# Stores in the third convolution, row terms between the two Hilbert products, and both copies of the mixed planes on ScalarE

## What is computed

```python
x = x + _L0_conv_ref(_gn(x), w_real, w_imag, b_real, b_imag)  # rfft2, complex 3x3 conv over frequencies + bias, irfft2
x = x + _L1_conv_ref(_gn(x))     # u, v: 8 channels each; gates: u . sum of v over rows > 0, v . sum of u over rows > 0
x = x + _L2_conv_ref(_gn(x), W)  # 3x3 convolution, 16 to 16 channels
x = x + _L3_conv_ref(_gn(x), weight)  # 3x3 convolution, 16 to 16 channels
```

## Time and profile before

| | |
|---|---|
| profiled execution, whole | 4709.38 us |
| its span, first to last instruction | 4707.6 us |
| median of three runs | 4704.55 us |
| PE busy | 4279.1 us, 91% |
| DVE busy | 3334.5 us, 71% |
| ACT busy | 2540.4 us, 54% |
| mean granted TensorE clock | 0.971 |

### The profile page before, as it was taken

One profiled execution on the slowest core, in us unless ns is written; L12 is line 12 of the kernel. 1 busy time (PEld: TensorE's weight loads), 2 busy tenths in 40 slices (PEclk: granted clock), 3 DMA queues, 4 the chain that ended last, 5 costly groups with the idle time before them and its releaser, 6 DMA issues.

```text
span 4707.6 us, 229463 instructions
## 1 busy us (share of the span) xinstructions
PE 4279.1 (91%) x85024; PEld 2675.9 (57%) x85024; DVE 3334.5 (71%) x13348; ACT 2540.4 (54%) x8637; POOL 1.0 (0%) x6
## 2 busy tenths in 40 slices
PE   4999988999999998999989999899998999988898
PEld 1455765556655566555655566555665557655476
DVE  2887757876578765887658875688756887578863
ACT  4675526655266543666436654366633666345562
POOL 0000000000000000000000000000000000000000
PEclk8999999999999999999999999999999999999999
DMA  7442015620155202651035510356003650034204
GB/s 190 130 136 76 4 40 171 189 89 4 49 185 182 74 3 62 187 186 54 3 85 183 183 38 3 94 181 187 27 3 108 186 181 14 3 109 139 88 4 146
DMA packets 290246, 468.06 MB, mean 99 GB/s; under 512 B 25536, under 2 KB 92288, under 8 KB 289408
## 3 DMA queue, kind: packets, MB, share of 16 engines
q1 hardware_dynamic: 289536, 457.92, 32.4%
HBM read 323.60 MB, written 134.22 MB: 97 GB/s over the span
## 4 chain that ended last, share of the span: by engine, by line
PE 60%; DVE 12%; DMA 8%; issue 8%; SPq 5%; ACT 3%; DVEq 1%; ACTq 1%
PE ps L1361 34%; PE ps L1255 9%; DMA raw<-x 8%; PE ps L1270 5%; PE ps L1263 3%; PE ps L1279 3%; PE ps L1125 2%; DVE shared L858 2%; SPq L426 2%; SPq L433 2%; DVE xin L853 1%; DVE shared L854 1%; SPq L407 1%; ACT x L584 1%; DVE xin L852 1%
## 5 line engine op out<-in xcount | busy, mean ns | idle before, releaser
L1361 PE MATMUL ps<-x,conv_s 32*32 32x512 f32 x49104 | 1741.9, 606 | 62.4 <-DVE x L1087 30.0
L1361 PEld LDWEIGHTS ps<-x,conv_s 32*32 32x32 f32 x49104 | 1242.5, 104 | 509.5 <-issue 273.7
L1255 PE MATMUL ps<-shared 32*32 32x512 f32 x16384 | 657.4, 604 | 0.0
L1270 PEld LDWEIGHTS ps<-hil,shared 128*128 128x128 f32 x4096 | 504.6, 194 | 194.0 <-issue 193.2
L662 ACT ACTIVATE x<-ps,vec 128x256 f32<-128x256 f32 x512 | 214.6, 470 | 741.4 <-PE ps L1361 741.4
L584 ACT ACTIVATE x<-ps,vec 128x128 f32 (+1 forms) x1024 | 377.6, 385 | 432.2 <-PE ps L1270 431.2
L858 DVE SCALAR_TENSOR_TENSOR shared<-xin,trig 128x128 f32<-128x128 f32 x2048 | 533.8, 301 | 106.7 <-DVE shared L854 98.8
L1279 PE MATMUL ps<-eye,vsb 128*128 128x128 f32 x2048 | 370.7, 305 | 237.1 <-DVE vsb L879 134.1
L1270 PE MATMUL ps<-hil,shared 128*128 128x128 f32 x4096 | 572.5, 284 | 0.0
L1086 DVE SCALAR_TENSOR_TENSOR x<-ps,x 128x256 f32<-128x256 f32 x512 | 214.8, 420 | 427.2 <-ACT x L662 426.2
L1255 PEld LDWEIGHTS ps<-shared 32*32 32x32 f32 x16384 | 310.3, 104 | 278.8 <-issue 213.2
(11 more groups left out here) (204 smaller groups left out, 4711.7 us busy)
## 6 DMA issues: line engine op xcount, KB each, us to landing
out<-x SPq DMA_DIRECT2D x512, 256.0 KB
shared<-x SPq DMA_DIRECT2D x448, 256.0 KB
raw<-x SPq DMA_DIRECT2D x256, 256.0 KB
raw<-x SPq DMA_DIRECT2D x512, 128.0 KB
shared<-t_strip SPq DMA_DIRECT2D x512, 96.0 KB, 4.0
x<-x SPq DMA_DIRECT2D x64, 256.0 KB, 8.8
x<-t_proj SPq DMA_DIRECT2D x1, 2048.0 KB, 11.8
trig<-t_trig SPq DMA_DIRECT2D x1, 512.0 KB, 12.1
```

The lines of the kernel that those rows point to most:

```text
L1255: mm = pe.matmul(ps[TM * cg:TM * cg + TM, bank, :], wst[TM * rg:TM * rg + TM, k, v, a, :], of[TM * rg:TM * rg + TM, :], start=(a == AXS), ...
L1270: mm = pe.matmul(quarter(ps[:, BY + 2 * odd + e, :], int(q < 2), q % 2), xt[:, e, q, :], hil[:, q, 0:P], start=False, stop=True, skip_grou ...
L1361: mm = pe.matmul(halves(ps[TM * cg:TM * cg + TM, banks[k], :]), conv_s[TM * rg:TM * rg + TM, kw, second, :], x1b[TM * rg:TM * rg + TM, of, ...
```

## The change

- SP: 8 strips of an image are stored in the next image's first layer, two in each of the first four steps (`DEFERRED`); 56 in its own third convolution, as each is evicted. The loads of the next image's pairs 0, 1 and 2 (pair 2 was loaded in the first layer) stand ahead of store 0, behind 36 and behind 48 stores (`STORED_BY`).
- VectorE makes planes for the next image one strip at a time, behind pairs 14, 17, 21 and 24, and within a strip waits for earlier results of its own a few instructions later.
- Both copies of the v bank are ScalarE's; VectorE's are gone. ScalarE copies the transposed bank out in one instruction (the identity for the transpose is turned by 32 columns instead), and before the eviction of the first strip, which now waits for a new semaphore of the row terms.
- TensorE: the row terms come between the two Hilbert products; a mix waits for the evicted banks one strip at a time, at its first matmuls of that strip; the counts of `keep_clock` change from 3, 3 and 2 to 2, 5 and 3.

```diff
@@ -27,7 +27,8 @@
 STORES = 16 * STRIPS // STORE_SEMS
-DEFERRED = STRIPS - 2 * UNROLL
+DEFERRED = 2 * UNROLL
+STORED_BY = (36, 48, STRIPS - DEFERRED)
 SIDE = HALF + 2
@@ -39,7 +40,7 @@
 RAW = 2
-U_AT, C_AT, PLANES_AT = (5, 8), (12, 14, 16), (20, 22)
+U_AT, C_AT, PLANES_AT = (5, 8), (12, 14, 16), (14, 17, 21, 24)
 DOT_CREDIT = 2
@@ -416,14 +417,13 @@
-            def store(i, s):
+            def store(i, s, k, turn):
...
                 sp.wait_ge(evicted, ev(i, 1 + STRIPS + s + 1))
...
-                sp.dma_start(out[i].rearrange("c (s r) w -> s r c w", r=ROWS)[s], x1[:, s, 0:N]).then_inc(c_stored[k], 16)
+                sp.dma_start(out[i].rearrange("c (s r) w -> s r c w", r=ROWS)[s], x1[:, bass.ds(s, 1), 0:N]).then_inc(c_stored[k], 16)
@@ -454,27 +454,27 @@
                     sp.sem_inc(s_sp, 1)
-                for pair in range(2, AHEAD):
-                    load_pair(i, pair, 2 * pair)
-                for pair in range(DEFERRED // 2):
+                for pair in range(PAIRS):
                     feed(pair, 2 * pair % TABLES)
-                    if stores_left:
+                    if stores_left and pair < DEFERRED // 2:
                         for e in range(2):
-                            store(i - 1, STRIPS - DEFERRED + pair * 2 + e)
-                for pair in range(PAIRS - UNROLL, PAIRS):
-                    feed(pair, 2 * pair % TABLES)
+                            s = STRIPS - DEFERRED + pair * 2 + e
+                            store(i - 1, s, s % STORE_SEMS, s // STORE_SEMS)
+                def stores(first, last):
+                    with sp.Fori(first // STORE_SEMS, last // STORE_SEMS) as j:
+                        for k in range(STORE_SEMS):
+                            store(i, j * STORE_SEMS + k, k, j)
                 if more:
-                    for pair in range(2):
+                    stored = 0
+                    for pair, until in enumerate(STORED_BY):
                         load_pair(i + 1, pair, 2 * pair)
-                for n in range(PAIRS):
-                    if more and n >= PAIRS - (STRIPS - DEFERRED):
-                        sp.wait_ge(evicted, ev(i, 1 + STRIPS + 2 * n + 2))
-                        sp.sem_inc(s_sp, 1)
-                        store(i, n - (PAIRS - (STRIPS - DEFERRED)))
-                    elif not more:
-                        for e in range(2):
-                            store(i, 2 * n + e)
+                        stores(stored, until)
+                        stored = until
+                else:
+                    stores(0, STRIPS)
@@ -573,12 +573,14 @@
                     flipped = ps[:, BX, :].rearrange("p (a b) -> p a b", a=4)
-                    nc.scalar.activation(xt[:, e, :, 0:P - TM], flipped[:, :, TM:P], ACT.Identity)
-                    nc.scalar.activation(xt[:, e, :, P - TM:P], flipped[:, :, 0:TM], ACT.Identity).then_inc(xt_ready, 1)
-                def evict(s, e, bank, k, turn):
+                    nc.scalar.activation(xt[:, e], flipped, ACT.Identity).then_inc(xt_ready, 1)
+                def evict(pair, e, bank, k, turn):
+                    s = pair * 2 + e
                     act.wait_ge(h_done, t0 + s + 1 + H_CREDIT)
+                    if e == 0:
+                        act.wait_ge(u_added, i * PAIRS + pair + 1)
                     act.wait_ge(c_stored[k], i * STORES + turn * 16 + 16)
@@ -588,8 +590,9 @@
                     act.wait_ge(mixed, i * PAIRS + pair + 1 + MIXED_CREDIT)
-                    act.wait_ge(turned, t0 + pair * 2 + T_CREDIT)
-                    nc.scalar.activation(vsb[:, 1, :], ps[:, BV + 1, :], ACT.Identity).then_inc(v_copied[1], 1)
+                    for e in range(2):
+                        act.wait_ge(turned, t0 + pair * 2 - 1 + e + T_CREDIT)
+                        nc.scalar.activation(vsb[:, e, :], ps[:, BV + e, :], ACT.Identity).then_inc(v_copied[e], 1)
@@ -608,9 +611,10 @@
                     copy_v(t)
+                    turned_out(t * 2, 0)
                     for e in range(2):
-                        evict(t * 2 - 2 + e, e, BY + 2 * (1 - odd) + e, 2 * (1 - odd) + e, uses)
-                        turned_out(t * 2 + e, e)
+                        evict(t - 1, e, BY + 2 * (1 - odd) + e, 2 * (1 - odd) + e, uses)
+                    turned_out(t * 2 + 1, 1)
                     squares(t * 2 - 2, 2 * (1 - odd), uses)
@@ -841,25 +845,28 @@
-            def make_planes(i, pair, slot):
-                for e in range(2):
+            def make_planes(i, pair, slot, strips=(0, 1)):
+                for e in strips:
                     s, k = pair * 2 + e, slot + e
...
                     plus, minus = xin[:, k, 0:HALF], xin[:, k, HALF:N]
-                    b.did(V.scalar_tensor_tensor(plus, raw[:, e, 0:HALF], v1(MEAN2), raw[:, e, HALF:N], ALU.subtract, ALU.add))
-                    V.tensor_tensor(minus, raw[:, e, 0:HALF], raw[:, e, HALF:N], ALU.subtract).then_inc(x_taken, 1)
-                    b.then(V.scalar_tensor_tensor(fg(wst[:, k]), fg(mix_s[:, 1]), row_trig[:, 0, bass.ds(s, 1)], fg(mix_s[:, 0]), ALU.mult, ALU.add))
-                    dve.wait_ge(x_taken, i * STRIPS + s + 1 + RAW)
+                    b.did(V.tensor_tensor(minus, raw[:, e, 0:HALF], raw[:, e, HALF:N], ALU.subtract))
+                    V.scalar_tensor_tensor(plus, raw[:, e, 0:HALF], v1(MEAN2), raw[:, e, HALF:N], ALU.subtract, ALU.add).then_inc(x_taken, 1)
+                    b.did(V.scalar_tensor_tensor(fg(wst[:, k]), fg(mix_s[:, 1]), row_trig[:, 0, bass.ds(s, 1)], fg(mix_s[:, 0]), ALU.mult, ALU.add))
+                    b.settle(but=1)
                     for a in range(2):
...
                                                          ALU.mult, ALU.mult, accum_out=gsum[:, 2 * a + q, bass.ds(s, 1)]))
+                        if a == 0:
+                            dve.wait_ge(x_taken, i * STRIPS + s + 1 + RAW)
                         ins = V.tensor_tensor(planes[:, a, k, HALF:N], plus, trig[:, a, 0:HALF], ALU.mult)
...
                             b.did(ins)
+                            b.settle(but=3)
                             b.did(V.scalar_tensor_tensor(fg(wst[:, k]), fg(mix_s[:, 2]), row_trig[:, 1, bass.ds(s, 1)], fg(wst[:, k]), ALU.mult, ALU.add))
@@ -1098,8 +1097,8 @@
                     if more and n in PLANES_AT:
-                        pair = PLANES_AT.index(n)
-                        make_planes(i + 1, pair, 2 * pair)
+                        s = PLANES_AT.index(n)
+                        make_planes(i + 1, s // 2, s - s % 2, (s % 2,))
@@ -1239,13 +1238,14 @@
                     due()
-                    pe.wait_ge(y_evicted, t0 + t * 2 - 2) if type(t) is not int or t > 1 else None
-                    due()
                     for e in range(2):
...
                         for e in range(2):
+                            if a == AXS and (type(t) is not int or t > 1):
+                                pe.wait_ge(y_evicted, t0 + t * 2 - 3 + e)
+                                due()
                             k = 2 * odd + e
@@ -1260,8 +1260,9 @@
                         pe.wait_ge(tab_loaded[table + e], (i * (STRIPS // TABLES) + uses + 1) * 16)
-                        pe.matmul(ps[:, BY + 2 * odd + e, :], strip[HP * e:HP * e + HP, table + e, 0:P], u[HP * e:HP * e + HP, :],
-                                  start=False, stop=False, skip_group_check=True)
+                        mm = pe.matmul(ps[:, BY + 2 * odd + e, :], strip[HP * e:HP * e + HP, table + e, 0:P], u[HP * e:HP * e + HP, :],
+                                       start=False, stop=False, skip_group_check=True)
+                    mm.then_inc(u_added, 1)
@@ -1289,10 +1290,11 @@
                     mix(t, odd)
+                    hilbert(t * 2 - 2, 0, 1 - odd)
+                    turn(t, 0)
                     add_u(t - 1, 1 - odd, table, table_uses)
-                    for e in range(2):
-                        hilbert(t * 2 - 2 + e, e, 1 - odd)
-                        turn(t, e)
+                    hilbert(t * 2 - 1, 1, 1 - odd)
+                    turn(t, 1)
                     project_next(2 * (1 - odd), table, uses, first)
@@ -1341,13 +1343,13 @@
                     prepare_z(i + 1)
-                keep_clock(3)
+                keep_clock(2)
...
                     prepare_h(i + 1)
-                keep_clock(3)
+                keep_clock(5)
@@ -1414,7 +1416,7 @@
                 statistics(G_OUT, vec[:, ST:ST + 2], stat[:, 0:2], gsel, P).then_inc(p_stat3, 1)
-                keep_clock(2)
+                keep_clock(3)
                 pe.wait_ge(v_conv3, i + 1)
```

25 lines of the change are left out of this document (9 added, 16 removed).

## The result

The changed kernel takes **4426.65 us** (median of four runs, 4420.08 to 4433.08) against 4706.13 for the kernel before on the same chip: a ratio of 0.941, 95% interval 0.939 to 0.943. The forecast was 4480, range 4390 to 4575. Its profiled execution took 4426.59 us, with a span of 4423.9.

The account below looks back on a forecast made before the run. First-layer steps were thought bound by TensorE's transpose-bank wait, with middle images slowed by stores, then by ScalarE; -14 - 180 - 26 + 6 - 7 = -221 from 4709.4 gave 4488, adjusted and rounded to 4480 us, range 4390 to 4575.

Parts of the forecast that it names:

- Order on both engines: First-layer step on TensorE and ScalarE: 0.71 us idle before the second transpose goes; 0.45 less per step, 14 us per image.
- So the step is bounded by ScalarE at 8.70 to 8.88 against TensorE's 8.58.: First-layer step: ScalarE's chain of evictions, copies and squares sets the new pace, taken as 8.80 us.
- Both copies on ScalarE: First layer: a copy costs 0.60 us on ScalarE against 0.69 on VectorE, already in ScalarE's chain; no separate gain.
- So the 21.0 us between the two come with the stores: First layer: images 1 to 6 exceed image 0 by 21.0 us through stores; moving 48 of 56 removes it, less 5.
- One of my own signs of being wrong: First layer: the prediction is wrong if VectorE still waits for inputs in mid-layer.
- inputs still land late: Rival, first layer: shorter steps keep half the excess, 6 x 10 us more than forecast, 4540; chance 0.07.
- supply waits of 5 to 8 us in each third convolution: Expected sign: TensorE waits that long for its instructions in each third convolution, with traffic near 140 GB/s.
- Start and first steps: First layer, images 1 to 6: 5 us of excess kept, 1.8 at the start and 0.8 for each of four store steps.
- Image 7: First layer of image 7: step from 9.2 to 8.2 us, 31 x 1.0 less 5 for eight stores, gain 26.
- Third convolution: Images 0 to 6: supply waits of 6.7 us come, TensorE waits of 5.9 leave; +0.8 each, +6 in all.
- Clock-keeping: One matmul fewer ahead of the second statistics saves 0.9 us per image, -7 in all; matmuls added elsewhere cost 0.

Follow-up runs that it names:

- ScalarE freed: Changed kernel with the squares of the next image cut from 512 to 16 columns on ScalarE in images 0 to 6: 4418.6 us (ratio 0.941).
- the first profile: First of two profiled executions of the unedited changed kernel: 4426.59 us, span 4423.9.
- the short stores: Changed kernel storing 16 of 512 columns per row, with as many store instructions and waits: 4379.1 us (ratio 0.933).

## Why the prediction was right, and where its steps were not

The total was 1.2% off, the gain 279 us for the 225 forecast. Two sizes that make it up were put on the wrong cause; that this does not show in the sum is luck, because the change contains both causes.

- *Order on both engines*, 14 us per image: image 0 gave 14.6. Undone on both engines it costs 19.5 per image. The working named the wrong half, though: with ScalarE's new order the row terms between the transposes are worth nothing in images 0 to 6 and 9 us in image 7, and ScalarE's order without them is enough. I had not set the emptying, 1.59 us after the transpose starts, against the Hilbert product plus the transpose's own 0.47, which already cover it but for a tenth.
- *"So the step is bounded by ScalarE at 8.70 to 8.88 against TensorE's 8.58."* The step is 8.7, but with ScalarE freed it stays there: TensorE's own work is 8.7 (its mix takes 3.41 us, 3.33 before, and its two transposes together 1.21 for 1.12). Why they are longer was not tested.
- *Both copies on ScalarE*, credited with nothing: alone they are worth 101 us. *"So the 21.0 us between the two come with the stores"* is the step that failed. Half of the 21 lies in the first six steps, and there moving the stores gave 1 of 11 us, where the copies gave 6. In the other 25 steps the stores make inputs late, but the time is lost through VectorE's order, plane and then copy: take away either and TensorE's wait goes. The stores alone are worth 36 us of the kernel before, and once the copy is gone no more than the 6 us that are not told from none. The change does both, so the sum came out. The Trainium skill's advice (TensorEngine Tiling (Array Packing), PSUM Bottleneck) to empty PSUM with both engines does not agree with the runs of this pair of copies: with VectorE taking one of them the kernel is 57 us slower.
- One of my own signs of being wrong came true: VectorE still waits for inputs in mid-layer (7.4 of image 2's 17.5 us lie behind its first 53 us). Of the rivals, "inputs still land late" had this observation right and the consequence wrong. Of the expected signs, supply waits of 5 to 8 us in each third convolution did not come either: the first profile has 0.5 to 4.4 in images 0 to 6.
- *Start and first steps*, 5 us kept: images 1 to 6 are 0.9 us over image 0. With this and the order term's 14.6, -208 for -180.
- *Image 7*, from 9.2 to 8.2 per step: its settled steps went from 8.93 to 8.46, -20 for -26. The 9.2 was a window of 32 mixes divided by 31, with a slow start in it; 9 of the 20 us come from the first six steps (58.5 to 49.3). The mix takes 4.23 us there, with 0.83 in which it stands still until the second eviction, for the 0.57 forecast.
- *Third convolution*, +6: by the first profile VectorE's waits fell by 27.5 us for 41 forecast, and TensorE's visible supply waits rose by 12 for 47. Together these are the -15 measured, but that is not the whole account: the bytes cost about 30 us in images 0 to 6, by the short stores, mostly without showing as a wait, so something else gave back what the waits do not show. That remainder is open.
- *Clock-keeping*, -7: worth 33. The way to the second convolution's first matmul got 5 us shorter, about as forecast. I priced what the matmuls ahead of the statistics held up, and put the two added behind at 0, "under VectorE's gates and weights". Nothing waits for them, but the clock at which the second convolution starts went with them.

## What to carry to other kernels

When an engine waits for a copy, look at what stands ahead of that copy on its engine and try moving the copy to an engine that has no late input ahead of it; moving the traffic that makes the input late cured only the later steps here. When an instruction's place is what makes another engine wait, test the order on one side alone before putting work between. A term that was put at 0 because nothing waits for it still has to be checked for what it does to the clock of the stage behind it.

## What the runs showed of the hardware

- 64 stores beside the third convolution cost TensorE 10.3 us in image 7 (110.8 against 100.5 with short stores), and its idle time in the window accounts for 6.0 of them; the granted clock is 1.00 in both. Traffic takes more from TensorE here than its waits show.
- Waits that the profile puts down to no engine ("issue") were for instructions: in the third convolutions all 18 over 0.3 us ended 2.28 to 2.49 us after a 16 KB packet of an instruction queue started.
- Ahead of the second convolution of image 1, 1.7 us more or less of matmuls without use, before an idle stretch of 1.15 or 2.79 us, went with a granted clock of 1.00 or 0.75 in its first 19 us. Over eight images the clock of the first 20 us is 1.00 every time with them and 0.74 to 1.00 without.
- After the jump in the loop over images, ScalarE waited 3.63 to 5.06 us for its own instructions with 16 stores just ahead (six images); with the stores spread over the stage the copy followed the mix after 2.41 to 3.37 us.
